# Relative attention: the output products in 32-row tiles, one batch pair each, and the weights turned by one transpose

## The reference, cut to what matters

```
q = k = (h @ Wq).reshape(I, B, H, F);  v = (h @ Wv).reshape(I, B, H, F)
content = einsum('ibnf,jbnf->ijbn', q + u_bias, k)
pos = left_shift(einsum('ibnf,jnf->ijbn', q + v_bias, r))
attn = softmax((content + pos) / sqrt_d, axis=j)
o = einsum('ijbn,jbnf->ibnf', attn, v).reshape(I, B, H * F)
x = x + o @ Wout + bout
```

## Time and profile before

| | |
|---|---|
| median of 3 runs | 825.94 us |
| profiled execution, its time | 827.49 us |
| its span in the profile | 825.7 us |
| granted TensorE clock, mean | 0.997 |
| PE busy | 792.1 us, 96% |
| VectorE busy | 523.7 us, 63% |
| ScalarE busy | 311.3 us, 38% |
| GpSimd busy | 301.0 us, 36% |

### The profile page before, as it was taken

One profiled execution on the slowest core, in us unless ns is written; L12 is line 12 of the kernel. 1 busy time (PEld: TensorE's weight loads), 2 busy tenths in 40 slices (PEclk: granted clock), 3 DMA queues, 4 the chain that ended last, 5 costly groups with the idle time before them and its releaser, 6 DMA issues.

```text
span 825.7 us, 16716 instructions
## 1 busy us (share of the span) xinstructions
PE 792.1 (96%) x6414; PEld 582.8 (71%) x6415; DVE 523.7 (63%) x1175; ACT 311.3 (38%) x827; POOL 301.0 (36%) x157
## 2 busy tenths in 40 slices
PE   4899999999989999999999999999999999999996
PEld 3555455555547778878876777688888888888883
DVE  5879777977755346776788877855473433343334
ACT  4312331233153427853267756723422112211211
POOL 0000000000062843543022222443639999993033
PEclk9999999999999999999999999999999999999999
DMA  9968556855502013040189000040475464541147
GB/s 342 382 238 319 201 207 234 319 205 208 211 32 103 1 51 106 3 128 7 53 287 375 3 0 0 2 153 1 178 275 204 159 203 155 185 143 51 55 119 259
DMA packets 46573, 127.00 MB, mean 154 GB/s; under 512 B 4001, under 2 KB 8353, under 8 KB 40369
## 3 DMA queue, kind: packets, MB, share of 16 engines
q1 hardware_dynamic: 36752, 105.44, 35.1%
q10 hardware_dynamic: 7200, 12.32, 4.3%
q0 software_dynamic: 2560, 8.39, 3.1%
HBM read 101.99 MB, written 24.15 MB: 153 GB/s over the span
## 4 chain that ended last, share of the span: by engine, by line
PE 78%; DVE 8%; DMA 6%; POOL 3%; ACT 2%; issue 2%; SPq 1%; another core or an unknown queue 0%; DVEq 0%; ACTq 0%; POOLq 0%
PE scores L592 11%; PE bank L625 8%; PE bank L1128 7%; PE bank L1130 7%; PE bank L1129 6%; DMA nat<-in_ctx_keys 5%; DVE ctxT L1820 2%; PE bank L682 2%; POOL picked L1370 2%; PE bank L836 2%; PE bank L684 2%; PE bank L683 2%; PE bank L842 2%; PE bank L837 2%; PE bank L872 2%
## 5 line engine op out<-in xcount | busy, mean ns | idle before, releaser
L1820 DVE STREAM_TRANSPOSE ctxT<-nat 128x1024 f32<-128x1024 f32 (+3 forms) x124 | 116.9, 1005 | 4.1 <-DMA nat<-in_ctx_keys 3.7
L625 PE MATMUL bank<-nat,probT 128*64 128x512 f32 (+1 forms) x416 | 94.4, 597 | 0.1
L592 PE MATMUL scores<-ctxT,hn 32*64 32x385 f32 (+5 forms) x2048 | 88.6, 487 | 3.5 <-DVE ctxT L1820 2.5
L1235 POOL TENSOR_TENSOR wq_lo<-wq_raw,wq_hi 128x1024 fp32r<-128x1024 f32 x4 | 9.5, 2402 | 223.3 <-ACT wq_hi L1461 223.3
L1357 POOL TENSOR_TENSOR ring_lo<-ring_raw,ring_hi 128x2048 fp32r<-128x2048 f32 x18 | 83.0, 4612 | 15.1 <-ACT ring_hi L1708 14.0
L592 PEld LDWEIGHTS scores<-ctxT,hn 32*64 32x64 f32 x2048 | 65.1, 131 | 24.2 <-issue 12.9
L1128 PE MATMUL bank<-ring_hi,xg_lo 128*128 x180 | 74.2, 412 | 0.4 <-DVE xg_lo L2440 0.4
L1130 PE MATMUL bank<-ring_hi,xg_hi 128*128 x180 | 70.6, 392 | 0.0
L1129 PE MATMUL bank<-ring_lo,xg_hi 128*128 x180 | 70.1, 389 | 0.0
L625 PEld LDWEIGHTS bank<-nat,probT 128*64 128x64 f32 (+1 forms) x416 | 28.8, 136 | 52.9 <-issue 51.4
L2452 DVE TENSOR_TENSOR rhm_lo<-bank,rhm_hi 128x512 fp32r<-128x512 f32 x21 | 14.5, 693 | 79.5 <-ACT rhm_hi L1719 75.9
(11 more groups left out here) (310 smaller groups left out, 1881.4 us busy)
## 6 DMA issues: line engine op xcount, KB each, us to landing
nat<-in_ctx_keys SPq DMA_DIRECT2D x48, 1024.0 KB, 7.6
ring_raw<-in_Wexp SPq DMA_DIRECT2D x21, 1024.0 KB, 6.2
x_slots<-zeros SPq DMA_DIRECT2D x1, 5632.0 KB, 17.6
y_slots<-zeros SPq DMA_DIRECT2D x1, 5632.0 KB, 32.3
hn<-x_slots ACTq DMA_DIRECT2D x22, 256.0 KB, 4.2
y_slots<-hn ACTq DMA_DIRECT2D x22, 256.0 KB
w_raw<-in_Wexp SPq DMA_DIRECT2D x3, 1024.0 KB, 5.3
nat<-in_ctx_keys SPq DMA_DIRECT2D x16, 130.0 KB
```

Of the source, the lines that this page charges most:

```text
L592: last = nc.tensor.matmul(scores4[64 * b:64 * b + 64, i, 0:keys_in[i]], q4[rows_i, j, 64 * b:64 * b + 64], ctxT[rows_i, b, j, 0:keys_in[i] ...
L625: last = nc.tensor.matmul(bank[7][64 * b:64 * b + 64, :], probT[0:n, j, 64 * b:64 * b + 64], nat[k % 2][0:n, b, j, :], start=j == 0, stop= ...
L1820: dve.transpose(dst, src).then_inc(columns_ready, 1)
```

## The change

The zero-padded block-diagonal tile goes. The turned weights take 256 columns, 32 for each head, and pair m has rows 32m to 32m+31: one transpose over 128 partitions writes all of them. An output product takes 32 rows of the array (the pair's values, 32x128) and 32 moving columns; there is one for each head and pair, the pairs in turn. Pair m writes to bank 4+m (last group: bank m), all eight heads next to each other. So a group fills half of each of four banks, and a group waits for the evictions of the one before it. ScalarE evicts pairs 0 and 1, VectorE pairs 2 and 3, each with two copies of 256 columns instead of one of 512, behind a single signal after the last product. At the end both high-part copies wait for both engines' evictions. GpSimd's clearing of the tile goes.

```diff
-        attT = [hn4[:, 2 * i:2 * i + 2, :].rearrange("p a (n q) -> p (a n) q", q=P) for i in range(2)]
+        attT = [hn4[:, i, 0:NH * PAIR].rearrange("p (n q) -> p n q", q=PAIR) for i in range(2)]
...
-        def output_bank(g, h):
-            return bank[2 + h] if g == NG - 1 else bank[4 + 2 * (g % 2) + h]
+        def pair_output(g, m):
+            return bank[m if g == NG - 1 else 4 + m][:, 0:NH * PAIR].rearrange("p (n q) -> p n q", q=PAIR)
+
+        def pair_places(g, m):
+            return (oT[:, :, g, :].rearrange("p n (i b) -> p n b i", b=GB)[:, :, 2 * m:2 * m + 2, :],
+                    pair_output(g, m).rearrange("p n (b i) -> p n b i", i=SEQ))
...
             def group_output(g, par):
                 pe.wait_ge(v_out, 2 * g + 2)
                 pe.wait_ge(attT_ready, g + 1)
-                if 2 <= g < NG - 1:
-                    pe.wait_ge(o_act, g - 1)
-                    pe.wait_ge(o_dve, g - 1)
+                if 1 <= g < NG - 1:
+                    pe.wait_ge(o_act, g)
+                    pe.wait_ge(o_dve, g)
                 for n in range(NH):
-                    last = nc.tensor.matmul(output_bank(g, n // 4)[:, (n % 4) * P:(n % 4 + 1) * P],
-                                            v_g[g % 3][:, n * F:(n + 1) * F], attT[par][:, n, :], start=True, stop=True)
-                    if n % 4 == 3:
-                        last.then_inc(o_full, 1)
+                    for m in range(P // PAIR):
+                        own = pair_rows(m)
+                        last = nc.tensor.matmul(pair_output(g, m)[:, n, :], v_g[g % 3][own, n * F:(n + 1) * F], attT[par][own, n, :],
+                                                start=True, stop=True, skip_group_check=True)
+                last.then_inc(o_full, 1)
...
-            pool.wait_ge(hT_full, NT)
-            nc.gpsimd.memset(hn4[:], 0.0).then_inc(attT_cleared, 1)
...
             def group_out(g):
-                act.wait_ge(o_full, 2 * g + 1)
-                nc.scalar.copy(oT[:, 0:4, g, :].rearrange("p n (i b) -> p n b i", b=GB),
-                               output_bank(g, 0)[:].rearrange("p (n b i) -> p n b i", n=4, i=SEQ)).then_inc(o_act, 1)
+                act.wait_ge(o_full, g + 1)
+                for m in range(2):
+                    last = nc.scalar.copy(*pair_places(g, m))
+                last.then_inc(o_act, 1)
...
             act.wait_ge(o_act, NG)
+            act.wait_ge(o_dve, NG)
             out_high(0, 0, slice(0, NH // 2), (0,))
-            act.wait_ge(o_dve, NG)
             out_high(0, 0, slice(NH // 2, NH))
...
-                for m in range(P // PAIR):
-                    own = pair_rows(m)
-                    last = dve.transpose(attT[par][own, :, own], att[g % 3][own])
-                last.then_inc(attT_ready, 1)
+                dve.transpose(attT[par], att[g % 3][:]).then_inc(attT_ready, 1)
 
             def group_out(g):
-                dve.wait_ge(o_full, 2 * g + 2)
-                dve.tensor_copy(oT[:, 4:8, g, :].rearrange("p n (i b) -> p n b i", b=GB),
-                                output_bank(g, 1)[:].rearrange("p (n b i) -> p n b i", n=4, i=SEQ)).then_inc(o_dve, 1)
+                dve.wait_ge(o_full, g + 1)
+                for m in range(2, 4):
+                    last = dve.tensor_copy(*pair_places(g, m))
+                last.then_inc(o_dve, 1)
...
             group_out(NG - 2)
+            group_out(NG - 1)
             dve.wait_ge(o_act, NG)
+            dve.wait_ge(o_dve, NG)
             dve.tensor_copy(o_hi[0][:, 0:NH // 2, BATCH:2 * BATCH].rearrange("p n (g b) -> p n g b", b=GB),
-                            oT[:, 0:NH // 2, :, GB:2 * GB]).then_inc(ohi_ready, 1)
-            group_out(NG - 1)
+                            oT[:, 0:NH // 2, :, GB:2 * GB]).then_inc(ohi_half, 1)
```

More of the change, by code:

```diff
@@ L317, in perceiver_kernel @@
         abias_ready, exp_ready, ainv_ready, att_ready = (sem(n) for n in ("abias_ready", "exp_ready", "ainv_ready", "att_ready"))
-        attT_cleared, pos_cleared, attT_ready, o_full, o_act, o_dve = (
-            sem(n) for n in ("attT_cleared", "pos_cleared", "attT_ready", "o_full", "o_act", "o_dve"))
+        pos_cleared, attT_ready, o_full, o_act, o_dve = (
+            sem(n) for n in ("pos_cleared", "attT_ready", "o_full", "o_act", "o_dve"))
+        ohi_half = sem("ohi_half")
         ohi_ready, olo_ready = sem("ohi_ready"), sem("olo_ready")
@@ L831, in out_product @@
                 first = isinstance(k, int) and k == 0
-                pe.wait_ge(ohi_ready, 2 if first else k + 3)
+                pe.wait_ge(ohi_ready, 1 if first else k + 2)
+                if first:
+                    pe.wait_ge(ohi_half, 1)
                 for n in range(NH):
                     if first and n == NH // 2:
-                        pe.wait_ge(ohi_ready, 3)
+                        pe.wait_ge(ohi_ready, 2)
                     nc.tensor.matmul(bank[6 + par][:], o_hi[par][:, n, :], wout_hi[:, n, :], start=n == 0, stop=False)
@@ L1275, in _ @@
                     weight_low(wout_lo, wout_raw, wout_hi, SPLIT["wout"], WOUT_PIECES[g - 1])
-            pool.wait_ge(ohi_ready, 2)
+            pool.wait_ge(ohi_ready, 1)
+            pool.wait_ge(ohi_half, 1)
             for t in kT_h + v_own:
@@ L1552, in _ @@
             group_out(0)
-            act.wait_ge(o_full, 2)
+            act.wait_ge(o_full, 1)
             values_out(3, 1, (0,))
@@ L2013, in group_turned @@
                 if g >= 2:
-                    dve.wait_ge(o_full, 2 * (g - 1))
-                for m in range(P // PAIR):
-                    own = pair_rows(m)
-                    last = dve.transpose(attT[par][own, :, own], att[g % 3][own])
-                last.then_inc(attT_ready, 1)
+                    dve.wait_ge(o_full, g - 1)
+                dve.transpose(attT[par], att[g % 3][:]).then_inc(attT_ready, 1)
             def group_out(g):
-                dve.wait_ge(o_full, 2 * g + 2)
-                dve.tensor_copy(oT[:, 4:8, g, :].rearrange("p n (i b) -> p n b i", b=GB),
-                                output_bank(g, 1)[:].rearrange("p (n b i) -> p n b i", n=4, i=SEQ)).then_inc(o_dve, 1)
+                dve.wait_ge(o_full, g + 1)
+                for m in range(2, 4):
+                    last = dve.tensor_copy(*pair_places(g, m))
+                last.then_inc(o_dve, 1)
             group_low(1, 1)
@@ L2046, in _ @@
             group_out(NG - 2)
+            group_out(NG - 1)
             dve.wait_ge(o_act, NG)
+            dve.wait_ge(o_dve, NG)
             dve.tensor_copy(o_hi[0][:, 0:NH // 2, BATCH:2 * BATCH].rearrange("p n (g b) -> p n g b", b=GB),
-                            oT[:, 0:NH // 2, :, GB:2 * GB]).then_inc(ohi_ready, 1)
-            group_out(NG - 1)
+                            oT[:, 0:NH // 2, :, GB:2 * GB]).then_inc(ohi_half, 1)
             def out_low(k, par):
-                dve.wait_ge(ohi_ready, k + 3)
+                dve.wait_ge(ohi_ready, k + 2)
+                if isinstance(k, int) and k == 0:
+                    dve.wait_ge(ohi_half, 1)
                 for i in range(2):
```

1 line of the change is left out of this document (removed).

## The result

The changed kernel takes 833.29 us (median of 5 runs, 831.22 to 836.24), the kernel before beside it 826.03 us (5 runs, 825.93 to 829.42). By the medians it is slower by 7.3 us; the ratio is 1.0077, 95% interval 1.0056 to 1.0098, which is 6.4 us. The forecast was +2.8. The direction is that of the forecast, the time lies inside the wide range (823 to 841) and outside the likeliest case's own (827 to 830.5). The profiled execution took 833.29 us with a span of 831.5 (before 827.49 and 825.7), so the traces are 5.8 us apart.

A forecast was written before the change was run, and what follows sets the result against it. PE was taken as the bound, busy nearly all the span. Terms 0.6 + 1.2 + 1.4 - 1.2 + 1.1 = +3.1, less restart, gave +2.8 on the 825.94 us median: 828.7 us, range 823 to 841.

The forecast's parts named there:

- likeliest case: The forecast itself, 828.7 us, given a chance of 0.50 and an own range of 827 to 830.5 us.
- Parts 1 and 2: Output matmuls at 29 ns an instruction, +0.6 us for eight groups; six exits from strip forms at 0.2 us, +1.2.
- Part 3: Banks reused one group earlier: PE stands 1.5 us at outputs of group 2 for ScalarE's eviction, +1.4 us.
- Part 4: Evictions: a strided half copy 0.68 us, two 1.27 on ScalarE, 1.24 on VectorE; beside PE in groups 0 to 6.
- Part 5: VectorE transposes: four of 0.43 us become one of 0.44, closing the 1.2 us hole before the last outputs, -1.2 us.
- the restart: Last outputs, now directly behind outputs of group 6, no longer pay 0.2 to 0.3 us for starting after a hole.
- Part 6: Tail: projection starts 1.9 us behind the last output instead of 0.8, as evictions wait for all products, +1.1 us.
- The clock: TensorE's granted clock, 1.00 in all four attention-stage windows, was taken as unchanged, with no term in the sum.
- A: Rival, cheaper loads: outputs take 0.7 us a group for 1.78; -3 us, 823 us; chance 0.14.
- B: Rival, row-strip loads serial at 106 ns, +40, 867 us; two at a time, +14, 840 us; chance 0.18.
- C: Rival, prices hide: exits between strip forms free, group 2's wait half met; 0 to +1.5, 826.7 us; chance 0.18.
- The bound of 2.4 us: Upper bound for the array's shape changes, if entering a strip form costs as much as leaving; +1.2 was taken.

The follow-up runs named there:

- a_fill: Changed kernel with unread full-array products in its two waits, six before outputs of group 2, seven before the projection; 827.57 us, ratio 1.0033 to the kernel before.
- a_evict: Changed kernel with ScalarE evicting group 1's outputs before the exponentials of group 3, not after; 829.73 us, ratio 1.0064 to the kernel before.
- b_inv: Kernel before with VectorE's inverse of group 7's sums moved ahead of its eviction of group 5; 822.76 us, ratio 0.9981 to the kernel before.
- a_outer: Changed kernel with the output products' two loops exchanged, eight heads of a pair in the same row strip consecutively; 893.31 us, ratio 1.0808 to the kernel before.

## Why the prediction was right in direction and short in size

*Parts 1 and 2, outputs and shapes.* 30 ns an instruction where 29 were forecast, +0.14 us a group for +0.08 behind full-array products; the price of leaving a strip form, however, was forecast for each of six exits, +1.2. The outputs behind the scores took 1.98 us before and take 1.95 to 1.99 now: the 0.2 of leaving the scores' form isn't paid when another strip form follows. It moved to the value products, whose first instruction now takes 0.43 (before, behind full-array outputs, 0.24). The two nearly cancel: a group's period grew by 0.13 us, and for groups 0 to 5 both parts together came to 0.9 instead of 1.7. The step that failed is the assumption that the outputs' own entry stays as dear as it was.

*Part 3, banks.* The wait came at group 2 and there alone, 1.67 us for the forecast's 1.5. That it comes so near is partly luck, for the errors cancel in it: PE came at 329.9 instead of 330.24, and ScalarE's copies ended at 331.34 instead of 331.75, but PE started 0.25 later still (the "issue" line), which had not been counted.

*Part 4, evictions.* A half copy was right (0.68 forecast, 0.668 measured), the pair too dear: 1.27 forecast, 1.11 measured in the mean. The overlap of neighbours is 0.16 us (VectorE) or 0.22 (ScalarE), not a tenth.

*Part 5 and the restart.* Outputs of 6 and 7 together went from 5.18 to 3.77 us, -1.4, for -1.2 and -0.3 with 0.16 for two groups' products. Transposes were 0.446 for 0.44.

*Part 6, tail.* From the last output to the projection 0.81 us became 1.89: +1.1, as forecast, but by luck in the parts: the copies took 1.08 for 1.27, and the latencies 0.4 for 0.2 (0.25 of it is the "issue" line).

*The clock.* "No longer pause of PE is added, so I change nothing for the clock" is the step of the forecast that failed. Even its premise was wrong, for the sum itself adds a wait of 1.5 and one of 1.9 us, and the earlier trace rows had shown a longest of 1.2. But the waits are the smaller part: put into the kernel before, both together cost 0.7 us of clock (0.0 to 1.5). The term put at nothing measured 3.15 us in the profile and 4 to 6 over all runs. Neither half alone reaches that: the waits around full-array outputs cost the 0.7 us just named, the row-strip outputs with full-array products in place of the waits (a_fill) 0.8 more than the kernel before (0.0 to 1.6). So it takes row-strip outputs and waits close together. With 32 rows and 32 moving columns at a time they take about as long as before, and PE reads "busy" for them, and yet the clock did not always hold. Two groups' outputs without a gap were enough in a_fill. At group 2 it fell with outputs(1), the scores of group 4, the wait and outputs(2) one behind the other, and in a_evict with a wait of 0.7 us in that place. Behind the outputs of groups 3, 4 and 5, each with a scores run before it and no wait, it held at 1.00. The full-array outputs of the kernel before, with the same waits, held it at two of four places. What each of strips, scores and waits contributes at group 2 was not taken apart, and the part of the 4 to 6 us beyond the two falls' 3.4 is in no trace.

*The rivals.* A is refuted by 30 ns a load. B's mechanism is real, 112 ns, but only for a loop order that the change doesn't have. C was wrong at group 2 and right in that going from one strip form to another is nearly free (the 64 outputs take 1.92 us behind full-array products, 1.95 or 1.96 behind scores); it would have given 826.7. The bound of 2.4 us, by which each entry costs as much as an exit, didn't come.

*What stays open.* 0.4 us of the two traces' 5.8 I can't explain. It arises in the last 18 us: at L1165 and its twin L1174 the difference still is 5.4 (808.17 and 813.58 us). The kernel before had medians from 823.66 to 827.12 in the comparisons, so only ratios are to be compared.

## What to carry to other kernels

Closing a 1.2 us hole by rewriting the products around it paid for the hole twice: a bank's reuse came one group earlier and the signal of a half was lost. Ask first whether an instruction in the queue ahead of the late one can be moved, as in b_inv. And count a tile's price not only in its own duration: where small-tile products follow each other, read the granted clock of the full-size ones behind them.

## What the runs showed of the hardware that was not expected

- Products on 32-row strips can lower TensorE's granted clock though PE is busy throughout: 1.00 at 363 us, 0.97 during 128 of them, 0.50 behind (a_fill); mean clock 0.953 with all of them in one strip's order (a_outer).
- The same wait of 2.0 to 2.1 us, outside the stage, was followed by a fall of the clock in nine of thirteen profiles (L608 at about 230 us); a fall cost 1.7 us.
- Products with a load of 128 columns: 112 ns one behind the other in the same row strip at 1.00 (213 at 0.50), 30 ns with four strips in turn.
- Going from one strip form to another cost at most 0.04 us; leaving it for the full array cost 0.2 us, once.
- Two strided copies of 256 columns out of the banks, back to back, take 1.11 us in the mean, no more than one of 512 (1.12).
- A 128x512 low part on VectorE mostly took 0.65 to 0.69 us, but 2.21 us and 2.74 us when a GpSimd subtraction of 2.4 us had begun before it, so the order of two engines off the critical path decided a wait of PE.
